# Four graph layers on one core: source one-hots of graph attention made during propagation, fewer blocks at the end, and five-slot low parts on VectorE

## The reference

```python
h = relu(layernorm(x)); x = x + propagate(h)      # 10 steps: out = 0.9 * spmm(out) + 0.1 * h
h = relu(layernorm(x)); x = x + graph_attention(h)
h = relu(layernorm(x)); x = x + dot_attention(h)
h = relu(layernorm(x)); x = x + mean_aggregate(h)
...
# graph_attention: hw = h @ W; e = leaky_relu(a_src[src] + a_dst[dst]); softmax of e over each dst
#                  out = tanh(sum over edges of hw[src] * alpha + bias)
```

## Time and profile before

| | |
|---|---|
| median of 3 runs | 1568.0 us (1566.27 to 1568.41) |
| profiled execution, its own time | 1561.12 us |
| its span, first to last instruction | 1559.3 us |
| mean granted TensorE clock | 0.893 of full speed |
| busy: PE, DVE, ACT, POOL | 80%, 79%, 37%, 23% of the span |
| propagation loop | 300.5 to 841 us |
| graph attention loop | 974.5 to 1182.8 us |
| dot attention loop | 1223.5 to 1459.2 us |
| last layernorm | 1464.4 to 1485.7 us |
| last product | 1490.8 to 1554.7 us |

### The profile page before, as it was taken

One profiled execution on the slowest core, in us unless ns is written; L12 is line 12 of the kernel. 1 busy time (PEld: TensorE's weight loads), 2 busy tenths in 40 slices (PEclk: granted clock), 3 DMA queues, 4 the chain that ended last, 5 costly groups with the idle time before them and its releaser, 6 DMA issues. The chain is left out here.

```text
span 1559.3 us, 45179 instructions
## 1 busy us (share of the span) xinstructions
PE 1244.0 (80%) x18543; PEld 1185.1 (76%) x18544; DVE 1234.2 (79%) x2306; ACT 583.3 (37%) x1271; POOL 355.8 (23%) x211
## 2 busy tenths in 40 slices
PE   4689888399999899998996400888883999999378
PEld 3278777399899899998995300888883899999378
DVE  6989888577677677676756899999996899999733
ACT  0057788200000000000000686566664677777311
POOL 1400000000000000000001010688882455555200
PEclk7868888699999999999998655999996999999689
DMA  0013334386678577676621474555534276775382
GB/s 11 0 61 115 121 114 141 104 334 266 225 272 287 208 277 275 219 262 251 245 73 54 154 261 161 213 213 213 213 130 193 89 270 263 279 283 221 141 332 90
DMA packets 88813, 297.54 MB, mean 191 GB/s; under 512 B 22399, under 2 KB 23976, under 8 KB 88604
## 3 DMA queue, kind: packets, MB, share of 16 engines
q1 hardware_dynamic: 66668, 231.86, 41.2%
q10 hardware_dynamic: 21600, 61.45, 10.3%
q0 software_dynamic: 336, 1.20, 0.3%
HBM read 188.31 MB, written 106.16 MB: 189 GB/s over the span
## 5 line engine op out<-in xcount | busy, mean ns | idle before, releaser
L1327 PE MATMUL psum<-work,count 128*128 128x192 f16 x6250 | 523.7, 248 | 35.7 <-issue 35.7
L1327 PEld LDWEIGHTS psum<-work,count 128*128 128x128 f16 x6250 | 521.6, 99 | 37.8 <-issue 36.9
L964 ACT ACTIVATE work<-work 128x1248 f32<-128x1248 f32 (+1 forms) x6 | 7.2, 1203 | 584.2 <-DVE work L947 584.1
L1672 PE MATMUL psum<-count 128*128 128x98 f16 x625 | 113.2, 209 | 114.6 <-DVE count L1726 99.2
L1718 POOL TENSOR_TENSOR count<-count 128x970 bf16<-128x970 f32 (+1 forms) x75 | 175.5, 2366 | 73.5 <-ACT count L1711 73.5
L1944 PE MATMUL psum<-count 128*128 128x100 f16 (+1 forms) x1875 | 176.6, 207 | 9.8 <-DVE count L2028 7.1
L1246 DVE SCALAR_TENSOR_TENSOR work<-psum,small,work 128x96 f32<-128x96 f32 x250 | 79.3, 317 | 123.7 <-PE psum L1327 123.4
L1945 PE MATMUL psum<-count 128*128 128x100 f16 (+1 forms) x1875 | 176.5, 207 | 0.1
L1944 PEld LDWEIGHTS psum<-count 128*128 128x128 f16 x1875 | 162.6, 98 | 14.8 <-DVE count L2028 11.1
L1945 PEld LDWEIGHTS psum<-count 128*128 128x128 f16 x1875 | 164.1, 98 | 0.2 <-issue 0.2
L2007 POOL TENSOR_TENSOR count<-count 128x1000 bf16<-128x1000 f32 (+1 forms) x75 | 133.1, 1775 | 108.2 <-ACT count L1993 108.2
(11 more groups left out here) (290 smaller groups left out, 2733.7 us busy)
## 6 DMA issues: line engine op xcount, KB each, us to landing
count<-onehots_by_src SPq DMA_DIRECT2D x75, 800.0 KB, 6.7
count<-bucket_rows_by_dst SPq DMA_DIRECT2D x50, 800.0 KB, 4.3
x<-bucket_rows_by_src SPq DMA_DIRECT2D x75, 400.0 KB, 5.8
onehots_by_src<-x ACTq DMA_DIRECT2D x75, 400.0 KB, 6.1
count_f<-count SPq DMA_DIRECT2D x25, 800.0 KB, 7.5
count<-count_turned SPq DMA_DIRECT2D x25, 800.0 KB, 5.6
count<-count_f SPq DMA_DIRECT2D x17, 800.0 KB, 4.2
count_turned<-x SPq DMA_DIRECT2D x25, 416.0 KB, 2.4
```

The costliest lines, as they stand in the source:

```text
L1327: last = nc.tensor.matmul(bank[i % BANKS], count16[:, j, i * P:(i + 1) * P], y[par][:, j, :], start=(j == 0), stop=(j == TILES - 1))
L1672: nc.tensor.matmul(ps[:, at:at + GW], node_hot[SRC][t % 2][:, s, :], high[:, s, :], start=True, stop=False, skip_group_check=True)
```

## The change

- `hot_by_dst` is a new DRAM tensor that holds the 25 source one-hots of graph attention. Propagation makes them: it has 50 more node pieces (150, and the same 50 edge pieces), each loaded from `by_dst`, compared and stored through the same four buffers. The 200 pieces are spread over 207 places, after tiles 0 to 22 of turns 0 to 8. A count tile is stored after every sixth node load.
- Graph attention loads the source one-hots (800 KB each) into four buffers. VectorE compares the destination ones after A's logits and makes the edge one-hot after B's; after C's it makes nothing.
- The low part of group C is subtracted by VectorE (`short_low`), after the edge one-hot and before it scales group A. GpSimd keeps A and B.
- `spot_next_round` is no block any more; what it did for further rounds stands at the end of the loops' own blocks.
- The last layernorm and the last product are one block, with semaphores in place of the barrier between them. The product's first half waits for the first half of the low parts only.

```diff
-                        q = 20 * turn + i - 1
-                        if turn < LAST and 1 <= i <= 20 and q % 6 < 5:
-                            spots.compare(dve, pieces, 5 * (q // 6) + q % 6)
+                        q = TURNS * turn + i
+                        if turn < LAST and i < TURNS and (q + 1) * pieces.total // SLOTS > q * pieces.total // SLOTS:
+                            spots.compare(dve, pieces, q * pieces.total // SLOTS)
...
+    source_hot = [node_hot[SRC][0], *(v.rearrange("p (t n) -> p t n", n=P) for v in spread[SRC]), node_hot[SRC][1]]
...
+    def load_source_hot(sp, t):
+        sp.dma_start(source_hot[t % SOURCES].rearrange("p t n -> p (t n)"), hot_by_dst[:, t, :]).then_inc(S["source_hot_%d" % (t % SOURCES)], 16)
...
                 for t in range(2, TILES):
-                    for i, v in enumerate((SRC, DST)):
-                        sp.wait_ge(S["node_hot"], 2 * (t - 2) + i + 1)
-                        load_spread(sp, k, t, v)
+                    sp.wait_ge(S["node_hot"], t - 1)
+                    load_spread(sp, k, t)
+                    if t + 2 < TILES:
+                        sp.wait_ge(S["gathered"], (t - 1) * PER)
+                        load_source_hot(sp, t + 2)
...
                 for i, (t, s0, n) in enumerate(groups):
-                    pool.wait_ge(S["high_done"], i + 1)
-                    after(pool, S["scattered"], i - LAG)
-                    nc.gpsimd.tensor_tensor(value_low[i % (LAG + 1)][:, 0:n * EW], ...
+                    if n > PER_BANK:
+                        pool.wait_ge(S["high_done"], i + 1)
...
                         if t + 1 < TILES:
                             if s0 == 0:
-                                spot_nodes(SRC, t + 1)
+                                spot_nodes(t + 1)
                             elif s0 == GROUP:
-                                spot_nodes(DST, t + 1)
-                            else:
                                 spot_edges(t + 1)
+                    if j >= 2 and groups[j - 2][2] == PER_BANK:
+                        short_low(j - 2)
...
         end_round(nc, [*S.values(), *m["spots"].all()])
-        spot_next_round(nc, m, pieces, k + 1, ids_dram, by_src, hot_by_src)
...
                 for j in range(TILES):
+                    for k, (t0, _) in enumerate(HALVES_OF_NODES):
+                        if s == 0 and j == t0:
+                            pe.wait_ge(low_made, k + 1)
                     last = nc.tensor.matmul(one_sums[s % 2], turned[s % READY][:, j, :], parts[:, j, :], start=(j == 0), stop=(j == TILES - 1))
...
-    with nc.Block() as block:
-        @block.sync
...
+    layernorm_relu(nc, m["norm"], x, h, sq, stats_of(m, "a"), stats_of(m, "b"), ready, sync=load_ahead, tensor=products, gpsimd=set_up, vector_before=dot_vector_end,
+                   vector_between=identity_and_inverse, vector_after=low_parts, scalar_after=scalar_end)
```

More of the change, by code:

```diff
@@ L968, in _, with __init__, load, compare @@
             scalar_after(act)
-def spot_next_round(nc, m, pieces, k, ids_dram, by_src, hot_by_src):
-    spots = m["spots"]
-    with nc.Block() as block:
-        @block.sync
[L976 to L996, removed]
+class NextRound:
+    def __init__(self, m, pieces, k, ids_dram):
+        self.m, self.pieces, self.k, self.ids_dram = m, pieces, k, ids_dram
+    def load(self, sp):
+        if self.pieces.edge is not None:
+            self.m["spots"].load_ids(sp, self.pieces, self.k, self.ids_dram)
+        for n in range(self.pieces.nodes):
+            self.m["spots"].load(sp, self.pieces, self.k, n)
+        self.m["spots"].wait_stored(sp, self.pieces)
+    def compare(self, dve):
+        dve.sem_inc(self.m["spots"].counted, 1)
+        for piece in range(self.pieces.total):
+            self.m["spots"].compare(dve, self.pieces, piece)
+        self.m["spots"].wait_stored(dve, self.pieces)
+    def store(self, act):
+        self.m["spots"].stores(act, self.pieces)
+        self.m["spots"].wait_stored(act, self.pieces)
 class Residual:
@@ L1105, in compare_edges, with stores @@
                                      pieces.ids[:, t0:t1, s, :].unsqueeze(2).broadcast_to(shape), ALU.is_equal).then_inc(self.made, 1)
-    def stores(self, act, pieces, hot_by_src):
-        for piece in range(PIECES):
+    def stores(self, act, pieces):
+        for piece in range(pieces.total):
             act.wait_ge(self.made, piece + 1)
-            if piece % 3 == 1:
-                s, half = divmod(piece // 3, 2)
+            if pieces.is_edge(piece):
+                s, half = divmod(pieces.edge_of(piece), 2)
@@ L1140, in propagate, with is_edge, edge_of, node_of @@
+    def is_edge(self, piece):
+        return self.per > 0 and piece % self.per == 1
+    def edge_of(self, piece):
+        return piece // self.per
+    def node_of(self, piece):
+        if not self.per:
+            return piece
+        group, i = divmod(piece, self.per)
+        return group * (self.per - 1) + i - (i > 1)
+def propagate(nc, m, ins, cnt_dram, cnt16_dram, ids_dram, by_src, by_dst):
     W = TILES * D
@@ L1277, in _ @@
             spots.load_ids(sp, pieces, 0, ids_dram)
-            for n in range(NODE_HALVES):
-                spots.load(sp, pieces, 0, n, by_src)
+            for n in range(pieces.nodes):
+                spots.load(sp, pieces, 0, n)
                 store_count_tile(n)
@@ L1296, in _ @@
         def _(act):
-            spots.stores(act, pieces, hot_by_src)
+            spots.stores(act, pieces)
         @block.tensor
@@ L1334, in large @@
             def large():
-                for piece in range(PIECES):
+                for piece in range(pieces.total):
                     spots.compare(dve, pieces, piece)
-                spots.wait_stored(dve)
+                spots.wait_stored(dve, pieces)
                 with dve.Fori(0, K_STEPS // 2) as kk:
@@ L1360, in propagate, with _ @@
     with nc.Block() as block:
+        @block.gpsimd
+        def _(pool):
+            clear_semaphores(nc, spots.all())
         @block.vector
@@ L1937, in _, with many @@
                         load_hot(sp, s, v)
+                def many():
+                    sp.wait_ge(S["added"], TILES)
+                    following.load(sp)
+                if_one(sp, m, None, many)
             @block.tensor
```

248 lines of the change are left out of this document (145 added, 103 removed).

## The result

The changed kernel takes 1625.5 us (median of 4 runs, 1622.7 to 1628.8) beside 1567.1 us for the kernel before in the same comparison (1563.0 to 1568.4). The ratio is 1.038, with a 95% interval of 1.036 to 1.041: 58 us slower. Forecast were 1611 us and a range of 1540 to 1640. The profiled execution has a span of 1620.9 us, 61.6 us more than the 1559.3 us of before.

The account below looks back on a forecast made before the run. It took TensorE to bound propagation and the port shared by VectorE and GpSimd to bound the graph attention loop. +13.0 - 1.0 + 41 - 4.2 - 6.2 = +42.6 us on 1568.0 gave 1611 us, range 1540 to 1640.

Parts of the forecast that it names:

- The side: Whole kernel: slower than before, given 0.72, against same 0.06 and faster 0.22.
- the two mechanisms: Propagation paced by node pieces' round trip through four buffers, +41 us; graph attention loop by the VectorE-GpSimd port, +13.0 us.
- the two gains at the end: Shorter wait behind dot attention, -4.2 us; earlier start of the last product, -6.2 us.
- the ring's pace: Propagation: round trip over four node buffers gives 3.43 us a node, 511 us for 149 steps, +41 us.
- The forecast's trip: Propagation: a node piece's load, compare, store and semaphore steps before its buffer is reloaded, 13.7 us.
- The upper end: Propagation: buffers also lose two tiles at each turn's end, 548 us, +78, kernel 1648 us; chance 0.12.
- The circle through the port: Graph attention loop: operations in series through the shared SBUF port take 8.67 us a tile against 8.13, +13.0 us.
- The start: Graph attention: one compare less before the first gather, -1.0 us.
- The ends: Behind dot attention -4.2 us, and ahead of the last product -6.2 us.
- The DMA engines are the limit: Propagation: DMA rate, not the buffers' round trip, limits; pieces need 451 us, stage stays free, 1569.6 us; chance 0.15.
- The port doesn't hold up the new order: Graph attention loop: GpSimd's subtractions fall into VectorE's pauses, 7.40 us a tile, -18 us, kernel 1580 us; chance 0.13.

Follow-up runs that it names:

- The ring of three: The changed kernel with three node buffers in propagation in place of four; 1697.0 us.
- the one of four without edge pieces: The changed kernel without the 50 edge pieces in propagation, 150 node pieces over four buffers; 1589.6 us.
- the kernel with the compares alone: The kernel before, with VectorE passing over every second node piece once more and no transfer added; 1566.1 us beside 1565.0.
- the kernel with the ends alone: The kernel before with only the two end edits, propagation and graph attention unchanged; 1556.8 us, ratio 0.994.
- three and five buffers: The changed kernel with three node buffers, 1697.0 us; the changed kernel without edge pieces and with five node buffers, 1569.5 us.
- the two kernels on the port: The changed kernel with the edge one-hot moved back behind C's reduction, 1608.8 us; or with GpSimd's ten-slot subtractions cut to one slot, 1609.4 us.
- the second trace of this kernel: The changed kernel run once more, unchanged; 1627.3 us, loop 226.2 us.
- the kernel with little on GpSimd: The changed kernel with GpSimd's ten-slot subtractions in the graph attention loop cut to one slot; 1609.4 us.
- the loop with the source one-hots alone: The changed kernel with source one-hots loaded, but all low parts on GpSimd and the edge one-hot behind C's reduction; 1589.7 us, loop 188.8 us.

## Why the prediction was right, and what in it was mis-sized

The side, the two mechanisms and the two gains at the end came out as forecast; the size was 15 us short.

**Propagation, +41 forecast, +57 measured.** The term that was mis-sized is the ring's pace. The forecast's trip was 6.4 + 6.5 us of landing, 0.6 of compare and an estimated 0.2 for two semaphore steps: 13.7 us. Measured are 6.3 + 5.8 + 0.6 as medians, and 14.3 in all, so 1.6 us lie elsewhere. By the program that is time in which a landed row waits while VectorE is at an update or waits for one, a made one-hot for the issue of its store, or a free buffer for the issue of its load; how it divides was not measured. The ring of three says the same (5.5 + 5.2 + 0.6 of 12.1, so 0.8 us), as does the one of four without edge pieces (5.8 + 5.5 + 0.6 of 13.4, so 1.5 us). The landings were taken a little too high, the holding time far too low: 3.57 us a node for 3.43, or 21 us over 149 steps. Of this 5 us came back: behind the last node compare 54.7 us of the stage are left (842.3 to 897.0) where before there were 59.5, which the forecast took as unchanged.

The forecast had nothing on the clock. Seen from TensorE, the same 57.3 us are 38 us more of waiting and 19 us of slower matmuls (busy 523.7, then 542.7 us, at a granted clock of 0.99, then 0.95). These are not to be added to the ring's 21 us: it is another division of the same time. Whether the stage would be shorter with the clock at 1.00 is open, since VectorE also waited for late products (63.8 us, 78 times), and that is part of what holds a landed row. The last section has the rows.

The upper end (ring also idle at the turns' ends, +78) was not reached. That VectorE's 50 compares would be hidden was right, as the kernel with the compares alone shows.

**Graph attention, +12 forecast, +15 measured.** The circle through the port was right: tiles in which the granted clock stays up take 8.4 to 8.7 us, 8.58 in the mean (forecast 8.67), the edge one-hot 2.84 us (2.9). The mean without the first two tiles is 8.71 us, since in four tiles the clock fell (last section); that it comes so close to 8.67 is luck. The compare is shorter than forecast, 1.68 us in the median against about 2: in the tile above it is issued 0.2 us later, and the port comes free 0.14 us earlier (1181.87 or 3.47 us after the scaling, forecast 3.61). That the whole comes within 3 us of the forecast is luck too, by errors that cancel. The line views of the edge one-hots, before and after:

```profile
L1733 DVE TENSOR_TENSOR count<-work,count x25: 1816/1912/2075, 976.5 to 1167.5; 128x3200 f16<-128x3200 f16 x25
```

```profile
L1780 DVE TENSOR_TENSOR count<-work,count x25: 1808/2843/3005, 1031.1 to 1234.8; 128x3200 f16<-128x3200 f16 x25
```

24 tiles of before take 191.0 us, 7.96 us each. The 8.13 us of the earlier trace rows are the longest in a pattern of 7.85 to 8.13. Reading one tile instead of the mean lost 4 us of the difference. Against that, the first two tiles after run in 5.2 and 6.9 us, while the circle is not yet closed, 3.6 us less than before. So the 24 spacings differ by 12.7 us. The start gives -1.0, as forecast, and the last tiles +3.3, which the forecast had not looked at: their last edge one-hot to the last add takes 18.6 us for 15.3.

**The ends, -10.4 forecast, -10.1 measured.** Both gaps closed to what was worked out, and the kernel with the ends alone gives the same 10 us by itself. The branches before the last add cost nothing behind dot attention; behind graph attention the gap grew from 0.96 to 1.39 us.

**The rivals.** "The DMA engines are the limit" fell with three and five buffers: the rate reached 305 GB/s, not the 355 of the rival, and one buffer more was worth 20 us at the same bytes. The rival is not wholly false: in the 2.9 us from 661.95 the share was 0.96 at 335 GB/s, and the trip grew with the load. "The port doesn't hold up the new order" fell with the two kernels on the port. What decided was the order of issue, GpSimd ahead of the compare by 0.95 us as worked out and by 1.17 as measured (1180.16 and 1181.33); busy time said nothing on it.

## What to carry to other kernels

In this case a ring of buffers had a pace of its own, the trip divided by the buffers; compare it with the pace that the schedule asks before adding pieces, and count in the trip the time in which a landed buffer waits for its engine. As long as both used the shared port, VectorE and GpSimd were as one engine: sum their operations, lay them in issue order, and put the long one where the other is idle; here a compare was taken off VectorE and a subtraction off GpSimd, and the loop still got longer by where the rest was put. Read a loop's period as a mean over the loop, not from one turn of it.

## What the runs showed of the hardware that was not expected

Behind a wait of TensorE the clock often fell, so that the wait may cost more than it lasts. In propagation after, TensorE waited 5.98 us, until 664.85, behind the sixth of the ten turns. Two windows behind that wait:

```profile
664.80:668.00 3.20, 3.15 (x20) 2.92 (x21) 0.57 (x3) 0.00 (x0) 0.00 (x0) 0.50 0.59 219
668.00:672.00 4.00, 4.00 (x46) 3.94 (x45) 2.80 (x8) 0.00 (x0) 0.00 (x0) 0.90 0.87 334
```

For 3.2 us the granted clock is 0.50, the lower level of 1.2 GHz, and only 20 matmuls run, half of what 3.2 us hold at 1.00 (487 in 40 us). If TensorE is what the stage waits for, this pause costs about 1.6 us more than it lasts, an estimate from these rows. The kernel before has such places too, but fewer: behind its pause of 3.95 us at 626.36, 23 matmuls ran in 3.3 us at 0.50, and of its four pauses three were followed by such a fall. After, it fell nine times in the stage. The same happens in the loop after, where TensorE idles in every tile (1.98 us before 1135.07):

```profile
1137.50:1138.50 1.00, 1.00 (x16) 1.00 (x14) 1.00 (x2) 0.56 (x3) 1.00 (x2) 0.50 0.36 138
1138.50:1139.50 1.00, 1.00 (x15) 1.00 (x14) 0.74 (x2) 1.00 (x6) 1.00 (x1) 0.50 0.00 0
```

There the clock falls in four of the loop's tiles. Those take 10.2 to 10.6 us, the next 7.4 to 7.5, together some 0.7 us more than two tiles of 8.6. In the second trace of this kernel there are seven such tiles, which is most of the 3 us by which its loop is longer. In the kernel with little on GpSimd it is the same: two tiles of 10.2 and 10.6 us beside 7.42, with a granted clock of 0.50 in windows of 2 us at 1120 and 1160. The loop of before, with no pause over 1.0 us from 984 on, stays at 1.00, and so does the loop with the source one-hots alone, with none over 1.0 us between 1041 and 1210. Not every pause of 2 us is followed by a fall: those of 1.97 us before 1082.68 and 1222.19 are not. That the pauses are the cause was read from the rows and not tested by an edit.
